# Gathers, denominators and rows of maxima issued from ScalarE's DMA queue

## What is computed

```python
xn = layernorm(x)
q, k, v = split(xn @ w_qkv)                      # 16 heads of 32
q, k = rope(rmsnorm(q, q_gamma)), rope(rmsnorm(k, k_gamma))
scores = where(causal, q @ k.T / sqrt(32), -1e30)
s = softmax(scores) @ v  ->  concat heads  @ w_out
gate, up = qlinear(xn, wq_gate), qlinear(xn, wq_up)   # int weights minus 128, times a scale; 1408 wide
g = silu(qlinear(silu(gate) * up, wq_down))
out = x + s * g
```

## Time and profile before

| | us |
|---|---|
| runs, median of 3 (lowest, highest) | 713.41 (711.95, 716.78) |
| the profiled execution | 715.66 |
| its span in the profile | 713.6 |
| granted TensorE clock, mean share of full speed | 0.983 |
| TensorE / weight load / VectorE busy | 658.2 / 557.8 / 556.3 |
| ScalarE / GpSimd busy | 445.4 / 397.0 |

### The profile page before, as it was taken

One profiled execution on the slowest core, in us unless ns is written; L12 is line 12 of the kernel. 1 busy time (PEld: TensorE's weight loads), 2 busy tenths in 40 slices (PEclk: granted clock), 3 DMA queues, 4 the chain that ended last, 5 costly groups with the idle time before them and its releaser, 6 DMA issues.

```text
span 713.6 us, 12527 instructions
## 1 busy us (share of the span) xinstructions
PE 658.2 (92%) x3670; PEld 557.8 (78%) x3670; DVE 556.3 (78%) x1370; ACT 445.4 (62%) x988; POOL 397.0 (56%) x594
## 2 busy tenths in 40 slices
PE   3589999889999999899999998999999989979997
PEld 2578887778888788788887887887878866757886
DVE  3778888899787868997878779978786787555674
ACT  2445666677676666876766768766756676643441
POOL 5544556587666665876666658765655574510000
PEclk9789999999999999999999999999999999989999
DMA  8244443524434233134343331144452424379882
GB/s 308 86 158 150 163 163 98 168 56 119 125 99 118 92 92 103 47 113 116 108 117 100 87 108 47 53 117 144 111 173 90 145 79 119 98 210 320 277 313 104
DMA packets 62530, 94.39 MB, mean 132 GB/s; under 512 B 12032, under 2 KB 24320, under 8 KB 62336
## 3 DMA queue, kind: packets, MB, share of 16 engines
q1 hardware_dynamic: 62464, 93.59, 42.4%
HBM read 59.09 MB, written 25.82 MB: 119 GB/s over the span
## 4 chain that ended last, share of the span: by engine, by line
PE 59%; POOL 14%; DVE 8%; issue 7%; DMA 6%; ACT 3%; SPq 1%; POOLq 0%; DVEq 0%; ACTq 0%
PE bank L1215 17%; PE bank L1112 13%; PE bank L1152 6%; PE bank L1191 5%; PE bank L1241 5%; PE bank L1240 5%; POOL rr L562 4%; PE bank L1173 4%; PE bank L1124 3%; PE bank L1137 3%; POOL pp L582 3%; POOL rb L571 2%; DMA wd_raw<-w_down 2%; POOL ra L568 2%; DVE bank L926 1%
## 5 line engine op out<-in xcount | busy, mean ns | idle before, releaser
L582 POOL TENSOR_SCALAR_AFFINE_SELECT pp<-pp 128x256 fp32r<-128x256 f32 x256 | 110.9, 445 | 141.1 <-DVE pp L904 140.7
L926 DVE CUSTOM_DVE_ANT_0 bank<-bank,msk_w 128x128 f32<-128x128 f32 (+3 forms) x256 | 121.1, 508 | 44.5 <-PE bank L1173 43.7
L562 POOL TENSOR_TENSOR rr<-ss,half 128x8 f32<-128x8 f32 x64 | 109.3, 1707 | 55.4 <-DVE ss L872 55.1
L904 DVE TENSOR_TENSOR pp<-pf,pp 128x512 fp32r<-128x512 f32 (+1 forms) x192 | 131.7, 686 | 7.3 <-ACT pp L691 7.2
L1112 PE MATMUL bank<-wq,xnt_h 128*128 128x384 f32 x512 | 116.6, 351 | 13.5 <-DVE qn L884 12.0
L690 ACT ACTIVATE pf<-bank 128x512 f32<-128x512 f32 (+1 forms) x192 | 100.6, 524 | 39.2 <-PE bank L1137 30.9
L1112 PEld LDWEIGHTS bank<-wq,xnt_h 128*128 128x128 f32 x512 | 92.2, 195 | 17.8 <-issue 14.2
L1215 PE MATMUL bank<-xnt_h,wgu 128*128 128x512 f32 x352 | 98.8, 402 | 7.3 <-DVE g L954 5.4
L1152 PE MATMUL bank<-pp,va 128*65 128x512 f32 (+3 forms) x512 | 99.0, 311 | 4.7 <-POOL pp L582 4.6
L691 ACT ACTIVATE pp<-bank 128x512 fp32r<-128x512 f32 (+1 forms) x192 | 101.0, 526 | 0.0
L1215 PE MATMUL bank<-xnt_l,wgu 128*128 128x512 f32 x352 | 96.5, 396 | 0.0
(11 more groups left out here) (78 smaller groups left out, 1169.2 us busy)
## 6 DMA issues: line engine op xcount, KB each, us to landing
wgu<-wg_dram SPq DMA_DIRECT2D x66, 256.0 KB, 3.1
hf_dram<-g SPq DMA_DIRECT2D x44, 256.0 KB, 3.2
hf_raw<-hf_dram SPq DMA_DIRECT2D x16, 512.0 KB, 6.5
wg_dram<-wgu SPq DMA_DIRECT2D x22, 256.0 KB, 3.0
xr<-x SPq DMA_DIRECT2D x16, 256.0 KB, 4.5
stage<-w_gu SPq DMA_DIRECT2D x16, 256.0 KB, 3.3
oh<-oraw SPq DMA_DIRECT2D x64, 64.0 KB, 1.9
ol<-oraw SPq DMA_DIRECT2D x64, 64.0 KB, 2.0
```

What stands on the lines that cost most here:

```text
L562: pool.tensor_tensor(rr[:, s, :], ss[:, s, :], half[:], ALU.pow).then_inc(rr_ok, 1)
L582: op = pool.affine_select(pp[:, :, a:a + P], pp[:, :, a:a + P], [[0, 2], [1, P]], ALU.is_ge, 0.0, base=0, channel_multiplier=-1)
L904: dve.tensor_tensor(pl[:, tile], pf[:, tile], ph[:, tile].bitcast(F32), ALU.subtract).then_inc(pl_ok, 1)
L926: op = dve.tensor_tensor_reduce(bank[:, a * w:(a + 1) * w], bank[:, a * w:(a + 1) * w], msk_w[:, N - w:N], 1.0, -3.0e38, ALU.add, ALU.max, ...
```

## The change

`gather`, `den_out`, `m0_out` and `m_out` move from SyncE's stream into ScalarE's. The DMAs, their waits and their semaphores are the same. They are issued at the end of ScalarE's beat, behind `square` and `o_high` and ahead of the splits of `SPLIT_HF`: at k = 3 first the maxima of head 0, at k = 0 first those of the other heads, then in every beat the gather of the head before, and behind a group's last gather the denominators. The waits of the gather for `o_ev` and for `os_ok` are now waits of ScalarE. `den_in` and `den_back` stay with SyncE.

```diff
@@ SyncE
-            def gather(i, h):
-                sp.wait_ge(o_ev, 4 * i + h + 1)
-                wait(sp, os_ok, i)
-                sp.dma_start(oh[HD * h:HD * h + HD, :], oraw[0:HD, h, :]).then_inc(og_in, 16)
-                sp.dma_start(ol[HD * h:HD * h + HD, :], oraw[HD:2 * HD, h, :]).then_inc(og_in, 16)
...
-                if k == 3 and there(16 * r + c + 4, NB):
-                    m0_out(r, c + 4, (c + 4) // 4 % 2)
-                if k == 3 and there(16 * r + c - 1, NB):
-                    gather(4 * r + (c - 1) // 4, (c - 1) % 4)
-                if k == 0 and c >= 0 and there(16 * r + c + 3, NB):
-                    m_out(r, c + 3, c // 4 % 2)
...
-                if k != 3 and there(16 * r + c - 1, NB):
-                    i, h = 4 * r + (c - 1) // 4, (c - 1) % 4
-                    gather(i, h)
-                    if h == HG - 1:
-                        den_out(i)
@@ ScalarE
+            def gather(i, h):
+                act.wait_ge(o_ev, 4 * i + h + 1)
+                wait(act, os_ok, i)
+                act.dma_start(oh[HD * h:HD * h + HD, :], oraw[0:HD, h, :]).then_inc(og_in, 16)
+                act.dma_start(ol[HD * h:HD * h + HD, :], oraw[HD:2 * HD, h, :]).then_inc(og_in, 16)
+            def den_out(i):
+                wait(act, rd_ok, i)
+                act.dma_start(den16[:], oraw[2 * HD:VW, :, :].rearrange("o h (a n) -> o (h a) n", n=HG * TB)
+                             ).then_inc(d_in, 16)
+            def m0_out(r, c, par):
+                wait(act, sm_ok, sm_count(r, c) + 3)
+                act.dma_start(qst[KS:KS + 1, par, 0:1, :].bitcast(F32).rearrange(
+                    "o h (t n) -> o (h t) n", t=TB), mrow0[:].bitcast(F32)).then_inc(m0_in, 16)
+            def m_out(r, c, par):
+                act.wait_ge(mt_ok, 4 * r + c // 4 + 1)
+                act.dma_start(qst[KS:KS + 1, par, 1:HG, :].bitcast(F32).rearrange(
+                    "o h (t n) -> o (h t) n", t=TB), mrow[:].bitcast(F32)).then_inc(m_in, 16)
@@ ScalarE, end of beat(r, c), behind square and o_high
+                if k == 3 and there(j + 4, NB):
+                    m0_out(r, c + 4, (c + 4) // 4 % 2)
+                if k == 0 and c >= 0 and there(j + 3, NB):
+                    m_out(r, c + 3, c // 4 % 2)
+                if there(j - 1, NB):
+                    gather((c - 1) // 4, (c - 1) % 4)
+                    if (c - 1) % 4 == HG - 1:
+                        den_out((c - 1) // 4)
                 for v in SPLIT_HF.get(c, ()):
                     high(v)
```

More of the change, by code:

```diff
@@ L413, in den_back @@
                     "h (o n) -> h o n", o=1).to_broadcast([HG, HD, N])).then_inc(rb_in, 16)
[L415 to L425, removed]
             def s_store(b, t):
```

## The result

| | before | changed |
|---|---|---|
| median of 4 runs, us | 714.63 | 789.02 |
| lowest to highest, us | 711.95 to 716.78 | 788.48 to 796.48 |
| span of the profiled execution, us | 713.6 | 787.4 |
| TensorE busy, us | 658.2 | 680.2 |
| ScalarE busy, us | 445.4 | 445.5 |

The ratio is 1.107, 95% interval 1.104 to 1.110: slower by 74 us, 10 us more than the 779 that was forecast and inside the range.

What follows compares the result with a forecast made beforehand. TensorE was taken as the bound, busy 658.2 of 713.6 us, with SyncE not short of time. The terms 51.4 + 10 + 12 - 7 + 0 made 66 us, put on the median of 713.41: 779 us, range 748 to 803.

Steps and rivals of the forecast that it cites:

- SyncE was not short of time: SyncE's queue waits 99.3 us for GpSimd's sum `on`, so relieving it buys TensorE nothing in the beats.
- Part 1: Beat boundaries: `mrow0` and `mrow`, issued behind `va`, land late and TensorE's scores wait; 51.4 us at 31 places.
- the prediction's bound for an early issue: Rows of maxima: if the issue starts with `va` and lands in 1.7 us, 14.6 us less, 37.
- 8.8 + 1.8: Boundaries with two gate halves: 0.55 us of stall, 16 times, 8.8 us; `o_high` ahead of `mrow0` on three, 1.8.
- Part 2: TensorE's clock: 6 of the 14 new waits of 2.4 to 2.9 us cost 1.7 us each; 10 us, ends 0 and 24.
- Part 3: Beat ends: issues and the wait for GpSimd's sum at k = 1 delay `t_high` and VectorE; 12 us, ends 0 and 25.
- ten others at 0.5 us: ScalarE's delay behind gathers: ten other beats at 0.5 us, besides four beats with k = 1 at 1.7 us.
- The end at 25 us: Upper end for ScalarE's delay behind its gathers, taken at 12 us; the lower end was 0.
- Part 4: Short stretches: while TensorE stalls, GpSimd and VectorE run on, so 7 of TensorE's 9.6 us idle come back.
- Part 5: Kernel's end: three issues before the `ht_h` splits cost 1.7 us, offset on SyncE's side; net 0, ends -1.7 and +1.7.
- The counterweight that was named: Kernel's end: SyncE no longer holds three `hf_raw` loads behind its gathers, and the 5.63 us write of `rd_dram` gets shorter.
- the prediction's own signs of being wrong: Line 1137 waits few or under 1 us, ScalarE issues much shorter, or TensorE more behind VectorE or ScalarE than these DMAs.

Runs made afterwards that it cites:

- SyncE's order alone: Kernel before, with only SyncE's order changed: in the last beat the three `hf_raw` loads go ahead of the last gather and `den_out`; 715.35 us, 1.002.
- the halves: Kernel before, with ScalarE issuing at its beat's end only `m0_out` and `m_out` (755.03 us, 1.053), or only `gather` and `den_out` (756.36 us, 1.055).

## Why the prediction was right, and where its sum was not

*SyncE was not short of time.* Right. With 176 issues taken off, its waits only moved to other lines (193 us for TensorE's gate halves, 107 us for VectorE's reciprocal), and TensorE won little by it: of its waits only `qn`, 7.2 to 5.8 us, and one for GpSimd's `pp`, 4.6 us to none, are smaller.

*Part 1, late rows: 51.4 us.* Right in mechanism and place, too large in size. TensorE waits 27.3 us in 20 places for them, the weight loads' line included up to some 39. Behind the end of `va` the scores start 1.49 us later in the boundary shown above, where 2.13 was taken. The step that failed is "the issue stands behind `va`": it was priced from `va`'s end, and the issue in fact starts 0.5 us ahead of it, while `square` and `va` are computed. That was the prediction's bound for an early issue, and more. At the 14 short boundaries the waits come to 25.2 us where 37.1 was taken, 1.8 us each. In the long beats the second gate half covers the landing: in half of the 16 the scores start 1.56 to 1.59 us behind `va`, as before, and the only waits, at six of them, make 2.0 us in all, where 8.8 + 1.8 was taken. Three of the six are the places where `o_high` goes ahead of `mrow0`. The landing itself was no constant: the longest wait, 3.08 us, ends with scores 3.5 us behind the start of the issue (178.40 to 181.88), against 2.0 in the boundary above. The whole half with its share of clock costs 0.053, 38 us, against 51.4 + 10.

*Part 2, the clock: 10 us.* Right in kind, low in size. Stretches of the changed kernel (length, TensorE busy, instructions, granted clock, DMA share, GB/s):

```profile
344.20:347.60 3.40, 1.57 (x8) 1.00 0.75 261
347.60:351.00 3.40, 3.40 (x17) 0.50 0.07 18
351.00:354.40 3.40, 3.40 (x24) 0.99 0.23 71
```

and the matmul that ends the wait in the first of them:

```profile
347.13 0.82 PE L1134 MATMUL bank<-qst,kst 97*128 97x512 f32 x3 [1.83 <-DMA qst<-mrow]
```

One wait of 1.83 us, and 3.4 us at 1.2 GHz behind it, 1.7 us of work lost, as priced. Over the span the lost share is (1 - 0.961) x 787.4 = 30.7 us against (1 - 0.983) x 713.6 = 12.1, 18.6 us more at full speed, and TensorE's busy time grew by 22.0 for the same instructions. The prediction let 6 waits of 14 cost that, and six falls do stand at or just behind waits for the DMA into `qst` (near 276, 310, 347, 442, 606 and 641 us). What its term lacked are the others: between 62 and 700 us the clock falls in 13 places, in the kernel before, its end apart, in one, and six of them stand behind waits for VectorE's `g` or `xnt_l` (near 125, 166, 334 and 498 us) or at one for ScalarE's `mrow` (near 429 and 593); the last, near 654, has one of either kind before it.

*Part 3, ScalarE behind its gathers: 12 us.* Here the sum was wrong by the most. The mechanism stood there, with the wait for GpSimd's sum at k = 1. In the changed kernel it is as predicted (timeline, 326 to 331 us):

```profile
326.62 1.27 POOL L553 TENSOR_TENSOR on<-oh,ol 128x512 f32<-128x512 f32 x1
...
327.98 0.54 ACTq L697 DMA_DIRECT2D oh<-oraw  x1
...
329.26 0.42 ACT L629 ACTIVATE tt<-qp 128x256 fp32r<-128x256 f32 x1 [2.70 <-issue]
...
331.30 0.41 PE L1121 MATMUL bank<-idr,tt 128*96 128x128 f32 x3 [2.37 <-DVE xnt_l L863]
```

But the term took "ten others at 0.5 us" for all other beats and let ScalarE's idle time absorb the rest. That is the step that failed: the gathers alone cost 0.055, 39 us with their clock, against 12. In the long beats behind k = 0 and k = 1 alone the table has +0.64 and +1.13 us for them. ScalarE's 38% of idle time is of no use there. It lies behind `t_high`, where ScalarE waits for TensorE, and not between `va` and `t_high`, where the way to TensorE's next gate half has 0.8 us to spare in a long beat. Three of ScalarE's waits before, over the whole span:

```profile
ACT kst L679 <- PE bank L1124: 45.0, 61, 3.0
ACT qst L674 <- PE bank L1124: 33.5, 40, 2.1
ACT pf L690 <- PE bank L1137: 30.9, 25, 2.0
```

The end at 25 us for this term was too low as well.

*Part 4, 7 us given back.* Not seen: the short stretches grew the most (the beats behind k = 0, 1 and 3 of the stretch from c = 24: 6.99, 7.68 and 7.47 us before, 9.31, 11.19 and 10.55 after).

*Part 5, the end: 0.* Right within its ends. The changed kernel's end:

```profile
700.86 0.59 ACT L662 ACTIVATE oraw<-bank 65x512 f32<-65x512 f32 x1 [1.72 <-PE bank L1149]
...
703.39 2.74 ACT L736 ACTIVATE ht_h<-hf_raw 128x1024 fp32r<-128x1024 f32 x3 [1.93 <-issue]
...
709.27 0.79 PE L1237 MATMUL bank<-wd,ht_h 128*128 128x512 f32 x1 [7.08 <-DVE yt L1045]
```

Three issues stand before the splits, and TensorE's wait grows from 5.19 us to 7.08; from the last `oraw` to the end of the span it is nevertheless 787.4 - 700.9 = 86.5 us against 713.6 - 626.0 = 87.6. The counterweight that was named is there: from the issue of the write of `rd_dram` to that of the DMA that reads it are 1.4 us (707.91 to 709.33), and the write took 5.63 before. That it is this which pays for ScalarE's issues is argued, not shown; SyncE's order alone, in the experiment above, won nothing.

So the direction and both mechanisms were right, and the total came near by luck, by errors of opposite sign: 51.4 + 10 + 12 - 7 in the prediction; from the halves, 38 for the late rows and 39 for ScalarE's holds, each with its part of the 18.6 us of clock. Of the prediction's own signs of being wrong one came true: TensorE stands behind VectorE and ScalarE more (37.7 + 7.6 us) than behind these DMAs (27.3). Counting only what is new since before, the two are about equal, 25.5 and 27.3 us.

An issue takes 0.53 to 0.81 us of ScalarE's sequencer, and ScalarE computes nothing meanwhile once the activations ahead of it are done. The Trainium skill (DMA: Bandwidth & Descriptors, "Where the ~2 µs actually goes") gives about 50 ns for the sequencer's dispatch, in a section on DMAs issued by GpSimd. As the price of a whole issue that is not borne out here; no run splits an issue into its parts.

## What to carry to other kernels

A DMA issue cost its engine's sequencer more than half a microsecond here, in order. Before it is put on a computing engine, find in the timeline how long that engine can be held at that very place before the bottleneck engine waits, and count all issues and waits that fall together there; the engine's share of idle time says nothing of it. A DMA that the bottleneck needs belongs where its data is ready, not at the end of a beat; here that alone was 0.053 against 0.006.

## What the runs showed of the hardware

- ScalarE's sequencer issues a DMA while earlier activations are computed: the issue at 316.70 ran beside `square` (316.69) and `va` (316.97). The first issue behind work is in part free: two small DMAs of 0.6 us each make a hold of 0.7 us, three 1.3 to 1.4 in most long beats.
- Small DMAs that nobody waits for, 0.6 us of issue each, are as dear as real ones once the free part is used up: the first 128 cost 10 us, 64 more 33, and another 64 45 us.
- The length of a wait of TensorE does not by itself say whether the clock falls. In the changed kernel waits of 1.83 us (to 347.13) and of 1.42 us (to 308.44) were followed by 3.4 us at a granted 0.50 and 0.53 (1.2 GHz); one of 3.08 us (to 181.88) was followed by 1.00 throughout the next 10 us, and before, one of 1.49 us by no fall either.
